# Moving the last query products ahead of the second probability turns, and masks and scores half by half, in a fused attention and mixture-of-experts kernel

## The chip, the cores and the metric

The kernel runs on one core of one Trainium2 chip. The metric is the device time of one execution in microseconds (us); lower is better. The profile is one execution of the same program, recorded by the hardware profiler.

## What is computed

`x` is 16 batches of 112 tokens of width 256. A cross-attention block against a context of 375 rows is added to `x` first. Then four layers follow. The part of a layer that matters here is causal self-attention with rotary positions, and after it a mixture of eight experts, of which each token uses two:

```python
for l in range(L):                       # L = 4, x is (16, 112, 256)
    h = rms(x) * ln1_w[l]
    q, k, v = h @ wq[l], h @ wk[l], h @ wv[l]     # 16 query heads, 4 key heads, head width 64
    q, k = rotate(q), rotate(k)                   # q * cos + rot_half(q) * sin
    a = softmax(q @ k.T / 8 + causal) @ v
    x = clip(x + a @ wo[l], -100, 100)
    h = rms(x) * ln2_w[l]
    comb = top_2(softmax(h @ wr[l]))              # 8 experts, 2 per token
    x = clip(x + sum_e comb[e] * ((silu(h @ wg[l][e]) * (h @ wu[l][e])) @ wd[l][e]), -100, 100)
```

## The kernel before, in words

Each engine has its own instruction list, written out by hand. Nothing is reordered; semaphores tie the lists together. Everything is float32, apart from the masks, which are bfloat16.

**A layer's attention** is a loop over the 16 batches on every engine (`iteration(b)` on TensorE and ScalarE, the loop `for b in range(B)` on VectorE, `attention(l)` on GpSimd). Projections are made for pairs of batches, `g = b // 2`. While pair `g` is attended, queries and keys of pair `g + 1` are projected: `heads_of(l, g + 1, m, bank)` (L819) makes key group `m = 0` and query groups 1 to 4. The even batch of a pair makes groups 0 and 1, the odd batch groups 2 (bank 0), 3 (bank 1) and 4 (bank 2). VectorE rotates each group (`rotate`: a shuffle L1628, two multiplications L1630 and L1632), and GpSimd adds the two halves of a query group (`add_rotated`, L594), which counts `g_rope`.

**One batch on TensorE**, in order: masks of heads 0 to 7 and of heads 8 to 15 (`causal`, L839, 4 matmuls each) and scores (`products`, L851, 16 matmuls each); the output projection of the batch before (`out_project`, L906, 16 matmuls); values (L827, even batches) or query group 2 (odd); the turns of probabilities 0 and 1 (`turn_probs`, L871, 4 transposes each, into banks 4 and 5); the turn of the residual rows (L891); the next projection; `turn_probs` 2 and 3, into banks 4 and 5 again; the router's logits (`route_logits`, L898); one more projection; in odd batches up to 11 the turn of the normalised input of pair `g + 2` (`norm_turn`, L810, into bank 4); and probabilities times values (`weigh`, L882).

`norm_turn` writes bank 4, so it waits until ScalarE has copied probability unit 2 out of that bank (`copy_probs`, L1300, which counts `a_pt`). `weigh` waits for the copies of all four units.

**One batch on VectorE**: the row maxima of each half of the scores (`maxima`, L1648), between them the sum of expert outputs for a later batch (`rows_in`, from the second layer on), the scaling of the first half of the probabilities (`scale_probs(b, 0)`, L1657 and L1658), the attention added to the residual (`add_attention`, L1663 and L1664), `scale_probs(b, 1)`, the rotations with the logits (`take_logits`, L1669) among them, and the two best experts (`top_two`). In batches 10 to 15 pieces of the routing come on top (`place_first`, `tiles_of_first` and others), which turn expert choices into row positions.

**One batch on ScalarE**: two output copies (L1304), 16 exponentials (L1291), the copies of turned probabilities (L1300), the copy of turned rows (L1317), in odd batches up to 11 the normalised input (`norm_in`, L1273), two more copies L1300, and a sum of squares (`square_out`, L1310).

**After the first nine batches** GpSimd scatters their rows to expert order in DRAM (L626, in batches 12, 13 and 14, between its additions L594). In batch 14 TensorE turns the first two expert tiles (`turn_tile`, L934), which SyncE loads once these scatters have landed.

## Time and profile before

| | |
|---|---|
| time before, median of 3 runs | 1882.78 us (1881.21 to 1884.82) |
| the profiled execution's own time | 1881.46 us |
| its span in the profile | 1879.6 us |
| TensorE (matmuls) busy | 1834.9 us, 98% of the span |
| VectorE busy | 1261.9 us, 67% |
| ScalarE busy | 950.8 us, 51% |
| GpSimd busy | 538.8 us, 29% |

A busy share says how much of the span the engine had an instruction in work. For TensorE, matmuls overlap and their ends are modelled, so the start of one group to the start of the next is the safer measure of what a group costs. The attention loops are at about 136 to 375 us, 570 to 806, 999 to 1235 and 1430 to 1666 us of the span; the expert tiles lie between them.

### The profile page before, as it was taken

To read this page: it belongs to the slowest core of one execution; us is meant where nothing else is said; L and a number is where in the kernel's file an instruction comes from. 1 tells how busy PE (TensorE), PEld (TensorE's weight loads), DVE (VectorE), ACT (ScalarE), POOL (GpSimd) and SP (SyncE) were. 2 spreads that over 40 slices of the span, in tenths; PEclk is the share of its full clock that TensorE was granted. 3 is DMA by queue.
4 is the path that set the end of the run, shared out by engine and by line. 5 is a ranking of instruction groups with operands and counts; after the bars stand their busy time and mean duration, and the time that the engine had idled before them with its cause. 6 is when DMAs were issued, how large, how long until landed. Compare 5 with 4: busy or idle time off the path is not lost.

```text
span 1879.6 us, 36506 instructions
## 1 busy us (share of the span) xinstructions
PE 1834.9 (98%) x10612; PEld 1360.0 (72%) x10613; DVE 1261.9 (67%) x3041; ACT 950.8 (51%) x3629; POOL 538.8 (29%) x721
## 2 busy tenths in 40 slices
PE   7999999999999999999999999999999999999995
PEld 5887888766668888766667888766667888865663
DVE  4676678754477878764566778764466778865456
ACT  4646777622226777732235777642224777752221
POOL 4652113440032332540032232531032332530024
PEclk9999999999999999999999999999999999999998
DMA  6423220256662330245562330235663431136566
GB/s 166 134 72 107 102 101 7 85 134 148 148 156 91 131 116 7 85 122 145 146 161 84 122 135 21 85 99 145 145 164 85 137 117 45 43 98 146 148 164 173
DMA packets 255292, 212.48 MB, mean 113 GB/s; under 512 B 145827, under 2 KB 226421, under 8 KB 255029
## 3 DMA queue, kind: packets, MB, share of 16 engines
q1 hardware_dynamic: 240808, 174.86, 33.8%
q0 software_dynamic: 13952, 35.33, 6.4%
q8 instruction: 82, 1.34, 0.3%
q14 instruction: 70, 0.57, 0.1%
q10 hardware_dynamic: 380, 0.38, 0.1%
HBM read 137.44 MB, written 73.05 MB: 112 GB/s over the span
## 4 chain that ended last, share of the span: by engine, by line
PE 87%; DVE 3%; DMA 3%; POOL 2%; ACT 2%; issue 2%; SPq 1%; POOLq 0%; DVEq 0%; ACTq 0%
PE ps L940 24%; PE ps L966 12%; PE ps L819 12%; PE ps L906 10%; PE ps L882 5%; PE ps L851 5%; PE ps L871 5%; PE ps L827 3%; PE ps L801 2%; ACT parena L1291 2%; PE ps L934 2%; PE ps L839 2%; PE ps L745 1%; PE ps L783 1%; PE ps L898 1%
## 5 line engine op out<-in xcount | busy, mean ns | idle before, releaser
L940 PE MATMUL ps<-arena,xeT 128*128 x1120 | 509.5, 593 | 0.0
L1291 ACT ACTIVATE parena<-ps,nmax 112x112 f32<-112x112 f32 x1024 | 345.5, 387 | 82.8 <-DVE nmax L1648 82.8
L940 PEld LDWEIGHTS ps<-arena,xeT 128*128 128x128 f32 x1120 | 210.2, 190 | 193.5 <-issue 187.3
L594 POOL TENSOR_TENSOR qk<-qk,rope 128x448 f32<-128x448 f32 x128 | 146.2, 1142 | 549.9 <-DVE rope L1632 549.8
L1345 ACT ACTIVATE parena<-ps,er 128x512 f32<-128x512 f32 x140 | 96.2, 687 | 375.6 <-PE ps L940 375.6
L819 PE MATMUL ps<-xnT,wqk_s 128*128 128x224 f32 x1280 | 273.5, 357 | 0.0
L573 POOL DMA_INDIRECT y_in<-sorted_y,pos x114 | 109.2, 958 | 499.6 <-DMA sorted_y<-tarena 397.4
L1291 ACT ACTIVATION_READ_ACCUMULATOR parena<-ps,nmax 112x1 f32 x1024 | 245.8, 240 | 0.0
L906 PE MATMUL ps<-wo_s,oT 128*112 128x256 f32 x1024 | 237.9, 385 | 1.3 <-issue 1.3
L819 PEld LDWEIGHTS ps<-xnT,wqk_s 128*128 128x128 f32 x1280 | 234.2, 191 | 2.4
L1932 DVE SCALAR_TENSOR_TENSOR parena<-parena,ps 128x512 f32<-128x512 f32 x140 | 96.1, 686 | 181.7 <-ACT parena L1345 181.6
L906 PEld LDWEIGHTS ps<-wo_s,oT 128*112 128x112 f32 x1024 | 175.7, 177 | 42.9 <-issue 2.0
L1648 DVE TENSOR_REDUCE nmax<-ps 112x8 f32<-112x896 f32 x128 | 136.8, 1086 | 58.7 <-PE ps L851 58.6
L626 POOL DMA_INDIRECT sorted_x<-x_sb,pos_x x128 | 124.2, 970 | 173.2 <-DVE pos_x L1855 139.5
L1335 ACT ACTIVATE xeT<-ps,ln2T 128x128 f32<-128x128 f32 x280 | 87.1, 364 | 170.5 <-PE ps L934 167.8
L966 PE MATMUL ps<-arena,tarena 128*128 x640 | 152.8, 382 | 2.3 <-issue 1.5
L1300 ACT ACTIVATE tarena<-ps 112x448 f32<-112x448 f32 x256 | 129.2, 574 | 37.4 <-PE ps L871 37.0
L1658 DVE TENSOR_TENSOR parena<-parena,rrec 112x896 f32<-112x896 f32 x128 | 139.8, 1092 | 4.4
L1934 DVE SCALAR_TENSOR_TENSOR parena<-parena,er,ps 128x512 f32<-128x512 f32 x140 | 104.7, 748 | 54.6 <-PE ps L940 54.0
L1304 ACT ACTIVATE oT<-ps 128x448 f32<-128x448 f32 x128 | 69.3, 545 | 120.7 <-PE ps L882 120.7
L966 PEld LDWEIGHTS ps<-arena,tarena 128*128 128x128 f32 x640 | 119.1, 195 | 14.8 <-issue 3.9
L851 PE MATMUL ps<-qk 64*112 64x112 f32 x2048 | 121.9, 262 | 0.0
(207 smaller groups left out, 2753.1 us busy)
## 6 DMA issues: line engine op xcount, KB each, us to landing
sorted_y<-tarena SPq DMA_DIRECT2D x140, 128.0 KB
xe<-sorted_x SPq DMA_DIRECT2D x132, 130.0 KB, 2.5
arena<-in_L_ffn_wg_dram SPq DMA_DIRECT2D x32, 512.0 KB, 3.7
arena<-in_L_ffn_wu_dram SPq DMA_DIRECT2D x32, 512.0 KB, 4.6
arena<-in_L_ffn_wd_dram SPq DMA_DIRECT2D x32, 512.0 KB, 5.6
hid_d<-tarena SPq DMA_DIRECT2D x240, 64.0 KB
tarena<-hid_d SPq DMA_DIRECT2D x60, 256.0 KB, 2.8
hid_d<-parena SPq DMA_DIRECT2D x240, 64.0 KB
```

The source lines that it names most:

```text
L573: pool.indirect_dma_start(out=y_in[:, b % 2, k, :], out_offset=None, in_=sorted_y[0:FIRST * SLOT, :] if b < PARTS[0][1] else sorted_y, in_ ...
L594: pool.tensor_tensor(q, q, rope[m % 2][:, :], ALU.add).then_inc(g_rope, 1)
L626: pool.indirect_dma_start(out=sorted_x if h == 0 else sorted_x[0:HROWS - WHOLE * SLOT, :], out_offset=bass.IndirectOffsetOnAxis(ap=pos_x[: ...
L819: last = pe.matmul(ps[:, bank, x * TN:x * TN + TN], wqk_s[:, k, n, :], xnT[:, g % 2, k, :], start=(k == 0), stop=(k == KD - 1))
L851: last = pe.matmul(score_out(b, p, j)[:, i, :], qT[g % 2][js, 4 * p + i, u * S:u * S + S], keys[g % 2][js, p, u * S:u * S + S], start=Fals ...
L906: last = pe.matmul(ps[0:S, 6, 0:D], oT[:, p, i * S:i * S + S], wo_s[:, 4 * p + i, :], start=(p == 0 and i == 0), stop=(p == 1 and i == 3))
L940: last = pe.matmul(ps[:, bank, :], xeT[u][:, k, :], w[:, bass.ds(e * 1024 + k * 512, 512)], start=(k == 0), stop=(k == KD - 1))
L966: last = pe.matmul(ps[:, 6, u * D:u * D + D], chunk, wd_s[:, bass.ds(e * 1024 + c * D, D)], start=(c == 0), stop=(c == 3))
L1291: last = act.activation(prob[:, n, :], ps[0:S, bank, h * S:h * S + S], ACT.Exp, bias=nmax[:, b % 2, n:n + 1], accum_out=rsum[:, b % 2, n:n ...
L1300: act.activation(probT[:, unit, :], ps[0:S, 4 + unit % 2, 0:GN], ACT.Copy).then_inc(a_pt, 1)
L1648: dve.tensor_reduce(nmax[:, b % 2, hs].rearrange("p (n h) -> p n h", n=2), heads(b, p), AX_X, ALU.max, negate=True).then_inc(d_max, 1)
L1658: dve.tensor_tensor(prob[:, hs, :], prob[:, hs, :], bc(rrec[:, hs], 2, [S, 8, S]), ALU.mult).then_inc(d_norm, 1)
```

## The change

In odd batches with a next pair, TensorE makes query group 4 and the logits before it turns probabilities 2 and 3. VectorE rotates group 2 before it scales the second half of the probabilities, then rotates group 3, takes the logits, and rotates group 4. ScalarE sums the squares before the second pair of copies. In all batches the masks and the scores go half by half; before, even batches up to 12 made both masks first and both halves of the scores after them. `place_first(1)`, in batch 11, comes after the second scaling instead of ahead of it.

```diff
@@ TensorE, iteration(b)
-                        together = not odd and b != B - 2
                         causal(b, 0)
-                        if not together:
-                            products(l, b, 0)
+                        products(l, b, 0)
...
                         causal(b, 1)
-                        if together:
-                            products(l, b, 0)
                         products(l, b, 1)
...
+                    if odd and more:
+                        pe.wait_ge(a_exp, l * 32 + 2 * b + 2)
+                        heads_of(l, g + 1, 4, 2)
+                        route_logits(b - 1)
                     turn_probs(b, 2)
                     turn_probs(b, 3)
-                    if b:
+                    if b and not (odd and more):
                         route_logits(b - 1)
-                    if more:
+                    if more and not odd:
                         pe.wait_ge(a_exp, l * 32 + 2 * b + 2)
                         if b:
-                            heads_of(l, g + 1, 4 if odd else 1, 2)
-                    else:
+                            heads_of(l, g + 1, 1, 2)
+                    elif not more:
@@ ScalarE, iteration(b)
+                    if odd and g + 1 < NP:
+                        square_out(b - 1)
                     copy_probs(b, 2)
                     copy_probs(b, 3)
...
-                    if b:
+                    if b and not (odd and g + 1 < NP):
                         square_out(b - 1)
@@ VectorE, the loop over b
+                    if odd and g + 1 < NP:
+                        rotate(step, l, g + 1, 2, 0)
+                    scale_probs(b, 1)
                     if b == RANK_STEP + 1:
                         place_first(1)
-                    scale_probs(b, 1)
...
                         if odd:
-                            rotate(step, l, g + 1, 2, 0)
+                            rotate(step, l, g + 1, 3, 1)
                         else:
                             rotate(step, l, g + 1, 0, 1 if b else 2, between=take_logits)
                     if b and (odd or g + 1 == NP):
                         take_logits(b - 1)
                     if g + 1 < NP:
                         if odd:
-                            rotate(step, l, g + 1, 3, 1)
+                            rotate(step, l, g + 1, 4, 2)
                         else:
                             rotate(step, l, g + 1, 1, 2 if b else 3)
-                    if odd and g + 1 < NP:
-                        rotate(step, l, g + 1, 4, 2)
```

## Rows read from the trace of the kernel before

**Rows 1.** The page's busy line: busy time, share of the span, instructions.

```profile
PE 1834.9 (98%) x10612; PEld 1360.0 (72%) x10613; DVE 1261.9 (67%) x3041; ACT 950.8 (51%) x3629; POOL 538.8 (29%) x721
```

**Rows 2.** Stretch view: batches 5, 6 and 12 (first layer), batch 12 (fourth).

```profile
core 0: us, PE busy (x) PEld busy (x) DVE busy (x) ACT busy (x) POOL busy (x), PEclk, DMA share, GB/s
214.62:229.22 14.60, 14.60 (x116) 12.50 (x114) 11.14 (x26) 10.50 (x46) 4.31 (x5) 1.00 0.32 109
229.22:243.69 14.47, 14.47 (x114) 11.86 (x112) 9.42 (x21) 10.87 (x47) 1.14 (x1) 1.00 0.31 110
317.45:332.24 14.79, 14.73 (x113) 11.77 (x112) 12.59 (x32) 10.47 (x45) 7.07 (x7) 1.00 0.14 41
1608.08:1623.10 15.02, 14.94 (x112) 11.74 (x110) 12.82 (x33) 10.48 (x45) 7.13 (x7) 1.00 0.13 40
```

**Rows 3.** Timeline of TensorE, batches 5 and 6: start, length, engine, line, count.

```profile
214.62 0.40 PE L839 MATMUL ps<-rows_b,causal_b 64*112 64x256 bf16 x4
...
216.74 3.71 PE L906 MATMUL ps<-wo_s,oT 128*112 128x256 f32 x16
220.28 1.68 PE L819 MATMUL ps<-xnT,wqk_s 128*128 128x224 f32 x8
...
222.80 1.69 PE L819 MATMUL ps<-xnT,wqk_s 128*128 128x224 f32 x8
224.33 0.93 PE L871 MATMUL ps<-cst,parena 112*112 112x112 f32 x8
225.10 0.47 PE L898 MATMUL ps<-wr_s,x2T 128*112 128x8 f32 x4
225.43 1.76 PE L819 MATMUL ps<-xnT,wqk_s 128*128 128x224 f32 x8
227.02 0.62 PE L810 MATMUL ps<-cst,xn 112*128 112x112 f32 x4
227.57 1.72 PE L882 MATMUL ps<-tarena,v_s 112*64 112x448 f32 x8
229.22 0.59 PE L839 MATMUL ps<-rows_b,causal_b 64*112 64x256 bf16 x8
229.65 1.85 PE L851 MATMUL ps<-qk 64*112 64x112 f32 x32
231.43 0.47 PE L906 MATMUL ps<-wo_s,oT 128*112 128x256 f32 x1
```

**Rows 4.** Timeline of GpSimd, end of batch 5: the addition of query group 4.

```profile
229.27 1.14 POOL L594 TENSOR_TENSOR qk<-qk,rope 128x448 f32<-128x448 f32 x1 [0.56 <-DVE rope L1632]
```

**Rows 5.** Timeline of ScalarE: copy of unit 2 alone, batch 5.

```profile
224.92 0.54 ACT L1300 ACTIVATE tarena<-ps 112x448 f32<-112x448 f32 x1 [0.21 <-PE ps L871]
```

**Rows 6.** Timelines, batch 0: ScalarE's copies and what they release on TensorE.

```profile
153.27 0.53 ACT L1300 ACTIVATE tarena<-ps 112x448 f32<-112x448 f32 x1
153.94 0.95 PE L871 MATMUL ps<-cst,parena 112*112 112x112 f32 x8 [1.26 <-ACT tarena L1300]
584.59 0.98 ACT L1300 ACTIVATE tarena<-ps 112x448 f32<-112x448 f32 x2 [1.32 <-PE ps L871]
585.62 0.20 PEld L882 LDWEIGHTS ps<-tarena,v_s 112*64 112x64 f32 x4 [0.56 <-ACT tarena L1300]
```

**Rows 7.** Timeline of VectorE, batch 5: second scaling and rotations 3 and 4.

```profile
222.83 1.09 DVE L1658 TENSOR_TENSOR parena<-parena,rrec 112x896 f32<-112x896 f32 x1
...
225.79 0.67 DVE L1628 STREAM_SHUFFLE rope<-ps 128x448 f32<-128x448 f32 x1
...
227.42 0.66 DVE L1628 STREAM_SHUFFLE rope<-ps 128x448 f32<-128x448 f32 x1
```

**Rows 8.** Timelines of VectorE and of TensorE's weight loads in batch 12.

```profile
319.47 1.09 DVE L1648 TENSOR_REDUCE nmax<-ps 112x8 f32<-112x896 f32 x1
323.44 0.70 PEld L827 LDWEIGHTS ps<-wv_s,xnT 128*112 128x112 f32 x4 [0.47 <-ACT parena L1291]
```

**Rows 9.** Timelines of GpSimd (batch 13) and TensorE (batch 14).

```profile
345.18 1.14 POOL L594 TENSOR_TENSOR qk<-qk,rope 128x448 f32<-128x448 f32 x1 [0.80 <-DVE rope L1632]
...
357.62 0.95 PE L934 MATMUL ps<-cst,xe 128*128 128x128 f32 x4 [0.32 <-DMA xe<-sorted_x]
358.51 0.97 PE L882 MATMUL ps<-tarena,v_s 112*64 112x448 f32 x4
```

## Prediction, made before the changed kernel ran

> **What bounds the kernel now.** The page's busy line comes first: TensorE has matmuls in work for 98% of the span, VectorE for 67% [rows 1]. That is a hint and no proof, so I read the stretches batch by batch, from the first mask of one batch to the first mask of the next. Batch 5 takes 14.60 us and batch 6 takes 14.47, and TensorE is busy for all of both, at granted clock 1.00 [rows 2]. The other engines rest for 3 us and more in each. So in a plain batch only two things move the time: what TensorE's own list costs from start to start, and a wait put into that list. VectorE, ScalarE and GpSimd matter only where they reach TensorE. Batch 12 shows the other kind: 14.79 us, 0.32 more than batch 6, and 15.02 in the fourth layer [rows 2]. All 64 batches follow these patterns; I count types and multiply.
>
> **Even batches, masks and scores half by half.** In batch 6 the 8 masks start at 229.22 and the output projection at 231.43: 2.21 us. In batch 5, which already goes half by half, the same 40 matmuls take 214.62 to 216.74: 2.12 us [rows 3]. No matmul is removed, so where are the 0.09? The second half of the scores needs GpSimd's addition of query group 4, which ends at 229.27 + 1.14 = 230.41 [rows 4]; the scores began at 229.65, and 16 of them at half of (231.43 - 229.65) would be through at 230.54. The first half at batch 5's pace would be through about 0.1 earlier. So the second half waits about 0.1 us for GpSimd. After the change the even batch does what batch 5 does, if group 4 is there in time: bounds 0 and 0.10 saved, I take 0.09 because the odd batch measures the same list. Six even batches a layer (2 to 12), four layers: 24 x 0.09 = 2.2 us saved. The wait on the first half is for groups 1 and 2, added long before. The maxima start earlier, but TensorE doesn't wait for them in plain batches: worth nothing.
>
> **Odd batches, order on VectorE.** Group 2's projection ends at 220.28 + 1.68 = 221.96 [rows 3], and a rotation occupies VectorE for 227.42 - 225.79 = 1.63 us [rows 7]. Ahead of the second scaling it runs from about 222.1 to 223.8; the scaling, which ended at 222.83 + 1.09 = 223.92 [rows 7], ends at about 225.1. The turn that waits for it used to start at 224.33; it now stands behind another projection of 1.53 (222.80 to 224.33) and the logits at 0.33 (225.10 to 225.43) [rows 3], so at 226.19. The scaling is ready 1.1 us before. Price if that cover were gone: up to 0.8 us a batch, the 225.1 against 224.33. Rotation 4 starts as soon as rotation 3 and the logits are taken, at about 226.8 instead of 227.42, so group 4 is added at about 229.7, while the next batch's second half of scores comes 1.2 us after a later batch start. No wait there.
>
> **Odd batches, order on TensorE.** Here I see a new wait. The turns of units 2 and 3 fill banks 4 and 5, and `norm_turn` fills bank 4 again. Before, logits and a projection (225.10 to 227.02, 1.92 us) lay between; after, nothing does. With S the start of the turns: ScalarE's copy of unit 2 started at 224.92, S + 0.59, and took 0.54 [rows 3, 5], so bank 4 is free at S + 1.13. TensorE would be through its eight turns at S + 0.77 (224.33 to 225.10) [rows 3]. The step from ScalarE's end to TensorE's start is bounded by batch 0: a copy from 153.27 of 0.53 ends at 153.80 and the turn starts at 153.94, 0.14 later; a pair that ends at 584.59 + 0.98 = 585.57 lets the weight load go at 585.62, 0.05 later [rows 6]. So `norm_turn` starts at S + 1.18 to S + 1.27.
>
> I cost the groups from the end of group 3's projection to `weigh` as a whole. Before, turns, logits, projection, `norm_turn`: 224.33 to 227.57, 3.24 us [rows 3]. After: projection 1.53, logits 0.33, then 1.18 to 1.27 to `norm_turn`, then its 0.55 (227.02 to 227.57) [rows 3]: 3.59 to 3.68. Logits followed by a turn instead of by a projection have no row; the projection behind the logits takes 1.59 (225.43 to 227.02) against 1.53, so up to 0.06 may hang on that junction. The difference is +0.35 to +0.50; I take +0.41, near the middle, as the longer step of 0.14 is that of the same pair of lines. Only odd batches 1 to 11 have a `norm_turn`: 6 x 4 x 0.41 = 9.8 us lost (8.4 to 12.0). Queued behind the wait are `weigh` and the next batch's masks and scores, so all of it is on the path. `weigh` itself isn't late: the second copy ends at about S + 1.6, and `weigh`'s units 2 and 3 start after S + 1.8. Batch 13 has no `norm_turn`: projection after projection saves the 0.06, 4 x 0.06 = 0.2 us.
>
> The Trainium skill, Perfetto Trace Analysis, section Matmuls, says that independent matmul groups should rotate through different PSUM banks, so that the copying out of one overlaps the matmuls of the next. It speaks against this edit, which lets two groups in bank 4 follow each other with one group between. Row and rule agree on the sign; the rule has no price, and without it the sum below is the same.
>
> ScalarE's sum of squares moves into time in which it waits for the turns: nothing.
>
> **Batch 12.** Its maxima start at 319.47, 2.02 us after the batch began at 317.45, while the first half of its scores would be done 1.2 us after that start at batch 5's pace. VectorE was behind with routing work, the exponentials followed late, and the values waited 0.47 us as a weight load [rows 8]. Since VectorE ends rotation 4 some 0.6 earlier against TensorE's list, and the batch starts 0.41 later, the delay goes, even with `place_first(1)` now uncovered (0.34): I expect 14.47 - 0.09. Beyond the 0.09 counted that is 0.32 in three layers (taking the first for them) and 0.55 in the fourth [rows 2]: 1.5 us saved (bounds 0 and 1.7).
>
> **Batch 14.** The expert tiles' turn starts at 357.62 after a wait for the load of `xe`, and ends only at 358.51: 0.89 for four transposes that cost about 0.55 as in `norm_turn`, with 0.32 or more of idle time ahead [rows 9]. The logits before them should take 0.33, and the whole is about 0.7 too long. The load waits for the last scatters, they for GpSimd, and GpSimd waited 0.80 us for VectorE's rotation 3 at 345.18 in batch 13 [rows 9]. That rotation comes about 0.77 earlier: it used to stand behind the scaling and rotation 2's own late start. So the scatters move 0.77 ahead and most of the wait goes: 4 x 0.68 = 2.7 us saved (bounds 0 and 3.0, as a transfer's time wanders).
>
> **Sum.** +9.8 - 2.2 - 0.2 - 1.5 - 2.7 = +3.2 us. The profiled execution took 1881.46 us for a span of 1879.6, so it would become 1884.7. It lies 1.3 below the median of the runs, 1882.78, against which the forecast is set: 1886.0 us. The expert part is untouched; its waits move with TensorE.
>
> **The rivals.** A difference of 0.2%, 3.8 us, is about what a measurement of this kernel can tell from no change.
> (a) The new wait, and nothing given back in batch 14: the tiles' load is bound by the DMAs and not by when the scatters were issued, and the junction costs its upper 0.06 too. For it: the load's time in the profile is that of two chained transfers. Against: GpSimd did wait on VectorE. 24 x 0.45 - 2.2 - 0.2 - 1.5 = +6.9: 1889.7 us. Chance 0.20.
> (b) The other side, faster: the wait at bank 4 isn't there, because ScalarE finds the copy ready sooner or TensorE's turns take longer behind the logits. Then the odd batch costs 0 and the savings stay: -6.6, 1876.2 us. It decides below 0.12 us of added time per odd batch, since 24 x 0.12 - 6.6 = -3.7. Against it stand the 0.59 and 0.54 of rows 3 and 5, which nothing in the change shortens. Chance 0.08.
> (c) A different wait: the scaling behind rotation 2 is late for the turns. It has 1.1 us of cover. If 0.2 of it showed in 28 odd batches, +5.6 on top: 1891.6. Chance 0.04.
> (d) Even batches keep their 2.21: +5.4, 1888.2. Chance 0.04.
> The forecast itself, within about 3 us of its time: 0.64.
>
> **How the numbers follow.** The forecast's own range, with the wait at its bounds (-1.4, +2.2) and the savings at theirs, is 1883 to 1889. To hold eight in ten it must reach (a) and most of (d) upward and allow the runs' spread downward: 1881.5 to 1891.0. Faster by over 0.2%: (b), 0.08. Slower: (a), (c) and (d), 0.28, and of the forecast the part above +3.8, which I put at 0.17 of its 0.64 although the centre is at +3.2, because a median of runs also moves by itself: 0.45 in all. Same: 0.47.
>
> **What the profile would show.** Right: in odd batches 1 to 11 a `norm_turn` (L810) with an idle bracket released by L1300, and 15.0 us for such a batch; even batches at 14.38; batch 12 without the weight load's wait; L934 in batch 14 with no or little wait for `xe`. Wrong: no bracket at L810, or one above 0.6 us; L871 waiting for L1658; the second half of an even batch's scores waiting for L594; batch 14 unchanged although L626 came earlier.

## The result, and the profile after

The changed kernel takes 1892.54 us (median of 9 runs, 1889.08 to 1897.17), the kernel before 1883.67 beside it (9 runs). The ratio is 1.0053, 95% interval 1.0041 to 1.0065. The forecast was 1886.0, with a range up to 1891.0: the sign was right, the size was not, and the time lies outside the range. The profiled execution took 1890.37 us for a span of 1888.5. It is 8.9 us longer than the span before, 1879.6.

The page's busy line of the changed kernel answers to [rows 1]:

```profile
PE 1838.0 (97%) x10612; PEld 1360.3 (72%) x10613; DVE 1276.7 (68%) x3041; ACT 950.8 (50%) x3629; POOL 542.8 (29%) x721
```

The instructions are the same in number, but VectorE is busy for 14.8 us more and GpSimd for 4.0 more. Nothing in the change gives them more work, so this line alone raises the question which of their instructions became longer.

The stretch view of the changed kernel shows batches 5, 6, 12 and 14 of the first layer, from first mask to first mask as in [rows 2]:

```profile
215.77:230.84 15.07, 14.82 (x116) 12.55 (x114) 11.97 (x27) 10.50 (x46) 4.57 (x6) 1.00 0.31 105
230.84:245.21 14.37, 14.37 (x114) 11.78 (x112) 9.27 (x19) 10.87 (x47) 0.89 (x1) 1.00 0.32 111
320.48:335.15 14.67, 14.62 (x114) 11.70 (x112) 12.52 (x31) 10.48 (x45) 7.03 (x7) 1.00 0.14 41
349.24:363.03 13.79, 13.10 (x109) 10.06 (x107) 7.36 (x21) 10.51 (x47) 7.62 (x8) 1.00 0.27 82
```

The granted clock (the share of full speed at which TensorE was allowed to run, the number before the DMA share) is 1.00 in all four, as before. I took the same difference for all 64 batches, after less before:

| batches (times four layers) | forecast, each | measured, each |
|---|---|---|
| 1, 3, 5, 7, 9 | +0.41 | +0.47 |
| 11 | +0.41 | +0.77 |
| 2 to 10, even | -0.09 | -0.10 |
| 12 | -0.41, in layer 4 -0.64 | -0.11, in layer 4 -0.36 |
| 13 | -0.06 | -0.05 |
| 14 | -0.68 | -0.06 in the mean (+0.02, -0.43, +0.11, +0.06) |
| sum of all 64 | +3.2 | +9.45 |

The rest of the 8.9 is scatter in the start and the expert parts. The plain batches came out nearly as forecast. Batches 11, 12 and 14 didn't: the first cost more than it should, and the other two gave almost nothing back.

TensorE's timeline in batch 5 of the changed kernel:

```profile
223.96 3.21 PE L819 MATMUL ps<-xnT,wqk_s 128*128 128x224 f32 x16
227.00 0.47 PE L898 MATMUL ps<-wr_s,x2T 128*112 128x8 f32 x4
227.32 0.95 PE L871 MATMUL ps<-cst,parena 112*112 112x112 f32 x8
228.53 0.73 PE L810 MATMUL ps<-cst,xn 112*128 112x112 f32 x4 [0.25 <-ACT tarena L1300]
229.19 1.72 PE L882 MATMUL ps<-tarena,v_s 112*64 112x448 f32 x8
```

This is the wait that was forecast, with the releaser that was forecast. From the start of the turns to `norm_turn` it takes 228.53 - 227.32 = 1.21 us (forecast 1.18 to 1.27). But from there to `weigh` it takes 0.66, where [rows 3] has 0.55. The list of waits (us in total, times, longest) has it in all 24 odd batches up to 11:

```profile
PE ps L810 <- ACT tarena L1300: 6.0, 24, 0.3
```

VectorE and GpSimd in the same batch show what was not forecast (the scaling is L1660 now):

```profile
225.18 2.02 DVE L1660 TENSOR_TENSOR parena<-parena,rrec 112x896 f32<-112x896 f32 x1
...
228.74 0.15 DVE L1671 COPY lg<-ps 112x8 f32<-112x8 f32 x1
```

```profile
225.11 1.13 POOL L594 TENSOR_TENSOR qk<-qk,rope 128x448 f32<-128x448 f32 x1 [6.84 <-DVE rope L1634]
```

The second scaling took 1.09 in [rows 7] and takes 2.02 here, in each odd batch up to 11. GpSimd's addition of group 2 starts 0.07 before it and ends at 226.24. The scaling ends at 227.20, 0.96 after that. It looks as if it did nearly nothing while the addition ran. The change itself brought them together: the rotation now ends right before the scaling, and the end of the rotation is what releases the addition.

In batch 14 the same instruction meets another one. GpSimd's and VectorE's timelines, and the chain that released the expert tile's turn:

```profile
353.58 0.94 POOL L626 DMA_INDIRECT sorted_x<-x_sb,pos_x  x1 [0.30 <-issue]
354.82 1.84 POOL L626 DMA_INDIRECT sorted_x<-x_sb,pos_x  x1 [0.30 <-issue]
```

```profile
354.77 1.09 DVE L1660 TENSOR_TENSOR parena<-parena,rrec 112x896 f32<-112x896 f32 x1
```

```profile
354.82 3.46 DMA sorted_x<-x_sb,pos_x
358.28 0.02 issue
358.30 2.11 DMA xe<-sorted_x
360.41 0.14 issue
360.54 0.91 PE ps L934 x4
```

The last scatter takes 1.84 us where the one ahead of it takes 0.94. It lands 3.46 after it was issued. Before, that was 2.78, with the scatter itself at 1.15. Here the scaling came first, and it looks as if the scatter had to stand behind it.

The Trainium skill, page "SBUF — State Buffer", section "Who interferes with whom", says that a VectorE `tensor_tensor` with both inputs in SBUF and a GpSimd instruction that reads SBUF want the same port pair, that whoever starts first has it for the whole instruction, and that the other does nothing meanwhile. The rows above have that form: 2.02 is 1.06 beside the addition and 0.96 after it. The rows show the times; that the operands are the reason had to be tested.

### The profile page after: what moved, and what is told of

It is laid out like the page before. It is cut to its first block, busy times and chain, and to the rows that moved or that the text cites. A ratio compares the mean times of both kernels' runs of the same rounds, so it can differ in the third digit from the quotient of the medians.

```text
span 1888.5 us, 36506 instructions
## 1 busy us (share of the span) xinstructions
PE 1838.0 (97%) x10612; PEld 1360.3 (72%) x10613; DVE 1276.7 (68%) x3041; ACT 950.8 (50%) x3629; POOL 542.8 (29%) x721
## 4 chain that ended last, share of the span: by engine, by line
PE 87%; DVE 4%; DMA 2%; issue 2%; POOL 2%; ACT 1%; SPq 1%; POOLq 0%; DVEq 0%; ACTq 0%
PE ps L940 25%; PE ps L966 13%; PE ps L819 11%; PE ps L906 11%; PE ps L882 5%; PE ps L851 5%; PE ps L871 4%; PE ps L827 3%; PE ps L801 2%; PE ps L934 2%; PE ps L839 2%; PE ps L745 1%; PE ps L783 1%; PE ps L810 1%; PE ps L898 1%
## 5 line engine op out<-in xcount | busy, mean ns | idle before, releaser
L819 PE MATMUL ps<-xnT,wqk_s 128*128 128x224 f32 x1280 | 266.6, 355 | 0.0
L1660 DVE TENSOR_TENSOR parena<-parena,rrec 112x896 f32<-112x896 f32 x128 | 162.0, 1266 | 4.4
L871 PE MATMUL ps<-cst,parena 112*112 112x112 f32 x1024 | 120.2, 260 | 2.5 <-ACT tarena L1300 1.3
```

What stands on the lines that cost most here:

```text
L819: last = pe.matmul(ps[:, bank, x * TN:x * TN + TN], wqk_s[:, k, n, :], xnT[:, g % 2, k, :], start=(k == 0), stop=(k == KD - 1))
L871: last = pe.transpose(ps[0:S, 4 + j, i * S:i * S + S], prob[:, p * 8 + j * 4 + i, :], ident[0:S, 0:S])
L1660: dve.tensor_tensor(prob[:, hs, :], prob[:, hs, :], bc(rrec[:, hs], 2, [S, 8, S]), ALU.mult).then_inc(d_norm, 1)
```

## The experiments

Sixteen runs were made, of fifteen kernels. In each, "before" is the kernel before on the same chip. Theory A is the wait for bank 4. The others are named as they came up; the letter G stands for one thing in experiment 2 and for another in experiments 10 and 11. Where batches are compared, all four layers are meant unless one is named.

**1. The halves alone.** The kernel before with the masks and scores of even batches half by half:

```diff
-                        together = not odd and b != B - 2
                         causal(b, 0)
-                        if not together:
-                            products(l, b, 0)
+                        products(l, b, 0)
...
-                        if together:
-                            products(l, b, 0)
```

> The kernel before with only the even batches' masks and scores half by half. Theory A (the loss is the new wait at bank 4, halves are a small gain): 24 even batches shorter by about 0.10 us, the batch stretch 14.36 or 14.37 instead of 14.47, odd batches unchanged at 14.60; in all 2.4 us less than before, a ratio of 0.9987, which the timing may just not resolve. Theory B (going half by half costs, for instance because the first half is now closer to its producers): even batches 14.47 or more, time not below before.

Measured: 1881.93 against 1882.87, ratio 0.9996 (0.9987 to 1.0005). The even batches 2 to 8 stay at 14.45 to 14.48, so the expected 14.37 didn't come. TensorE's timeline of batch 6 in this run:

```profile
230.43 0.36 PE L839 MATMUL ps<-rows_b,causal_b 64*112 64x256 bf16 x4
230.64 1.04 PE L851 MATMUL ps<-qk 64*112 64x112 f32 x16
231.61 2.63 PE L906 MATMUL ps<-wo_s,oT 128*112 128x256 f32 x11
```

The second half of the scores takes 0.97 to the output projection where batch 5 of the kernel before takes 0.90 (215.84 to 216.74). The output projection still starts 2.21 after the batch, as before, and GpSimd's addition of group 4 still starts 0.05 after it and ends at 1.18. The halves cost nothing and give nothing.

**2. The moves alone.** The changed kernel with the even batches' masks and scores in their old order (the diff above, reversed).

> The changed kernel with the even batches' masks and scores as they were before (both masks first). The run with halves alone moved nothing, so theory F (the 0.10 us that even batches gained comes from query group 4 being added sooner, which the moved rotations bring, and not from the halves) expects 14.37 in even batches here too, odd batches at 15.07, and the time of the changed kernel. Theory G (it takes both edits together) expects even batches at 14.47 and 2.4 us more than the changed kernel.

Measured: 1892.94 against 1884.47, ratio 1.0047 (1.0033 to 1.0061). The even batches are 0.11 shorter here too, with the old order; the odd ones are at +0.47 and +0.77. GpSimd's addition of group 4 starts 0.25 ahead of batch 6 instead of 0.05 after it. So the 0.10 of the even batches is real and comes from the rotations that end sooner, not from the halves. The halves are worth nothing in either kernel. One layer differs: in the first, batch 14 is at -0.71. There the last scatter started 0.04 after the scaling instead of 0.06 to 0.10, and it took 0.93 and the scaling 1.16. Whether batch 14 gives its 0.7 back hangs on some hundredths here.

**3. GpSimd's addition after the scaling.** The changed kernel, in odd batches:

```diff
                             if odd and m == 2:
+                                pool.wait_ge(d_norm, l * 32 + 2 * b + 2)
                             add_rotated(l, g + 1, m)
```

> The changed kernel, but GpSimd's addition of query group 2 waits until VectorE's second scaling of that odd batch is done. Theory C (the 2.02 us of that scaling, 1.09 before, come from GpSimd's addition running beside it): the scaling falls back to 1.09 in all odd batches, VectorE is 0.9 us earlier behind it, batch 11 loses its extra 0.30 us (15.38 to 15.08), batch 12 loses its wait of about 0.30 (14.67 to 14.37), plain odd batches stay at 15.07. Sum 4 x 0.6 = 2.4 us less than the changed kernel. Theory D (the scaling is slow for another reason, such as the rotation just ahead of it): it stays at about 2.0 us and nothing moves.

Measured: 1892.19 against 1882.87, ratio 1.0042 (1.0028 to 1.0055). VectorE and GpSimd in batch 5 of this run:

```profile
227.57 1.09 DVE L1662 TENSOR_TENSOR parena<-parena,rrec 112x896 f32<-112x896 f32 x1
```

```profile
228.74 1.14 POOL L594 TENSOR_TENSOR qk<-qk,rope 128x448 f32<-128x448 f32 x1 [8.10 <-DVE parena L1662]
```

The scaling is back at 1.09. In all four layers batch 11 falls from +0.77 to +0.47, and batch 12 from -0.11 to -0.41 (in the fourth from -0.35 to -0.65). Together that is the 2.4 us that theory C expected. The plain odd batches stay at 15.07 and batch 14 stays as it was. So the long scaling accounts for batches 11 and 12, and it does nothing in the plain odd ones while the wait for bank 4 stands there.

**4. The turned rows in bank 3.** The changed kernel with the wait for bank 4 taken away: `norm_turn` writes bank 3, whose scores have been read by then, ScalarE copies it at the end of the odd batch, and the next batch's second masks wait for that copy.

```diff
-                        pe.wait_ge(a_pt, l * 64 + b * 4 + 3)
+                        pe.wait_ge(a_exp, l * 32 + 2 * b + 2)
                         for k in range(KD):
-                            norm_turn(l, g + 2, k, 4, k * TN)
+                            norm_turn(l, g + 2, k, 3, k * TN)
...
```

> The changed kernel, but the turn of the normalised input goes to bank 3, whose scores are used up, and ScalarE copies it out at the end of the odd batch instead of in the next one. Theory A (the loss is the wait for bank 4): the wait at L810 is gone, odd batches 1 to 9 fall from 15.07 to about 14.55, 24 x 0.5 = 12 us less than the changed kernel, so 2 to 4 us below the kernel before. Theory E (the loss is the moved projection or the new neighbours on TensorE, not the bank): odd batches stay near 15 us. If the copy out of bank 3 is late for the next batch's masks, even batches show a wait of a few tenths at L839.

Measured: 1892.07 against 1882.87, ratio 1.0047 (1.0034 to 1.0061). TensorE in batch 5 of this run:

```profile
227.66 0.96 PE L871 MATMUL ps<-cst,parena 112*112 112x112 f32 x8
228.46 0.64 PE L810 MATMUL ps<-cst,xn 112*128 112x112 f32 x4
229.33 1.72 PE L882 MATMUL ps<-tarena,v_s 112*64 112x448 f32 x8 [0.24 <-issue]
```

`norm_turn` follows the turns after 0.80 and waits for nothing. But `weigh` now waits: it overwrites the bank of the logits, and VectorE, held up by its long scaling, takes them only at 229.08 to 229.23. The plain odd batches cost +0.27 instead of +0.47. A second wait stood 0.2 us behind the first. The 12 us that theory A expected became 4.0 by these batches, and the time shows even less; in the profiled execution batch 14 of the fourth layer is 2.9 us longer than before (see what stays open).

**5. Both.** Experiments 3 and 4 in one kernel.

> Both of the last two edits. Theories A and C together: odd batches about 14.55 with batch 11 like the others, even batches 14.37 with batch 12 like the others; about 14 us below the changed kernel and 4 to 6 us below the kernel before, ratio to before about 0.997. If the two costs are not separate (the freed time is lost to the same wait), it is no faster than the one with bank 3 alone.

Measured: 1881.36 against 1882.87, ratio 0.9993 (0.9984 to 1.0002). The odd batches are at 14.57, 0.03 below the kernel before, the even ones 0.10 below, batch 12 0.24. The 64 batches sum to -1.9 where the changed kernel had +9.45. In batches 1 to 13, which the fourth layer's batch 14 doesn't blur, it is -4.3 against +9.6: 13.8 us less. There the two edits alone gave 2.4 (experiment 3: 0.6 per layer in batches 11 and 12) and 4.0 (experiment 4: 0.20 in each of 20 plain odd batches). So the whole loss is gone with the two together, and more than half of it goes only so. The expected ratio of 0.997 was missed for two reasons. Batch 12 gets 0.24 and not the 0.41 of experiment 3: batch 11 is 0.50 shorter, so VectorE is nearer to being late, its maxima start 1.78 after the batch (1.32 in experiment 3), and the values wait 0.34. And batch 14 gives nothing back and is 2.65 longer in the fourth layer. The same kernel ran again beside experiment 9:

> The same kernel as bank3_pool, beside late_scaling_14 on one chip, so that the two are compared directly. By the earlier run: ratio to before 0.9993, all odd batches at 14.57, batch 14 as before.

Measured: 1881.17 against 1882.77, ratio 0.9991 (0.9982 to 0.9999). The batches repeat, apart from batch 14: +1.50, +1.08, +0.01 and +1.05.

**6. Logits between the turns and `norm_turn`.** The changed kernel with `route_logits` behind `turn_probs(b, 3)` in all batches.

> The changed kernel, but the router's logits come back between the last two turns and the turn into bank 4 (odd batches). Theory A (the wait is for the copy of unit 2 out of bank 4): the 0.33 us of the logits fill most of it, the idle time at L810 falls from 0.25 to about 0 and plain odd batches from 15.07 to 14.75 or a little above, since the logits are then taken later by VectorE; 24 x 0.3 = 7 us less than the changed kernel at most. If the next wait behind it (the probabilities times values waiting for the logits to be taken) takes over, odd batches stay within 0.15 of 15.07. Theory E (no wait, only dearer neighbours): no change.

Measured: 1889.86 against 1884.47, ratio 1.0031 (1.0021 to 1.0040). The plain odd batches stay at +0.42. TensorE and VectorE in batch 5 of this run:

```profile
225.81 3.21 PE L819 MATMUL ps<-xnT,wqk_s 128*128 128x224 f32 x16
229.10 0.98 PE L871 MATMUL ps<-cst,parena 112*112 112x112 f32 x8
229.92 0.47 PE L898 MATMUL ps<-wr_s,x2T 128*112 128x8 f32 x4
230.33 0.73 PE L810 MATMUL ps<-cst,xn 112*128 112x112 f32 x4
```

```profile
227.03 2.02 DVE L1659 TENSOR_TENSOR parena<-parena,rrec 112x896 f32<-112x896 f32 x1
```

The logits fill 0.33 of the time in which bank 4 is awaited: from the turns to `norm_turn` it is still 1.23. But the turns start 3.29 after the projections instead of 3.04, since the scaling ends at 229.05 and they come 0.33 sooner than in the changed kernel. With the scaling at 1.09 they would have gone 0.25 earlier. In batch 13, with no `norm_turn` to fill, `weigh` now waits 0.30 for the logits (+0.28).

What the plain odd batches gain over the changed kernel (0.05 each), batch 13 loses again. This kernel's ratio is 1.0031 where the changed one had 1.0053, and that is batch 14: it is at -0.71, -1.14, -0.69 and -0.71. GpSimd and VectorE in the first layer's:

```profile
356.33 0.93 POOL L626 DMA_INDIRECT sorted_x<-x_sb,pos_x  x1 [0.30 <-issue]
```

```profile
356.81 1.09 DVE L1659 TENSOR_TENSOR parena<-parena,rrec 112x896 f32<-112x896 f32 x1
```

The last scatter starts 5.04 after the first mask of batch 14, where the changed kernel has 5.58, and so 0.48 ahead of the scaling (0.34 in the fourth layer). It keeps its 0.93, and the expert tile's turn waits for nothing. Nothing is left out of this kernel and the operands are the same: only the order in which the two instructions start has changed.

**7. The cover taken away.** TensorE has the order of the kernel before, VectorE and ScalarE that of the changed one, so that the scaling stands behind rotation 2 and no projection 4 covers it.

> TensorE's odd batches in the order of before (turns, logits, projection of group 4, turn into bank 4), halves in all batches, VectorE and ScalarE in the order of the changed kernel. Rival (c) of the prediction: the rotation ahead of the second scaling makes the turns of units 2 and 3 wait, because nothing covers it. With the scaling at 2.02 us, ended at 12.6 us less its start (about 11.4 us after the batch began) against turns at 9.7, the wait is 1.5 to 1.7 us in each of 28 odd batches, about 40 us over the kernel before; with a scaling of 1.09 it would be 0.8 and 22 us.

Measured: 1926.63 us in a single run, span 1924.8. TensorE in batch 5:

```profile
228.96 1.69 PE L819 MATMUL ps<-xnT,wqk_s 128*128 128x224 f32 x8
232.24 0.98 PE L871 MATMUL ps<-cst,parena 112*112 112x112 f32 x8 [1.59 <-DVE parena L1656]
```

The turns start 3.28 after the projection instead of 1.53: 1.75 late, and the whole is 42 us over the kernel before, where about 40 was expected. In batch 13, where the scaling takes 1.09, they are 0.83 late. That is the "0.8" that the prediction gave as the price of the lost cover. It is right where the two engines don't meet and less than half where they do.

**8. The scaling of batch 14 left out.** The changed kernel in which the first half of batch 14's probabilities is not multiplied by its reciprocals (that part of the computation is left out).

> The changed kernel without the multiplication that scales the first half of the probabilities in batch 14 (that half stays unscaled, so the output is not the reference's). Theory H (the last scatter before the expert tiles takes 1.84 us instead of 1.15 because VectorE's scaling, which reads two SBUF operands, runs beside GpSimd writing its descriptors): the last L626 of the first nine batches falls to about 0.95, its data land about 0.9 us sooner, TensorE's wait at L934 goes and batch 14 is about 0.7 shorter (13.8 to 13.1). Rival (the scatter is long for its DMA or its rows): it stays at 1.8.

Measured: 1887.98 us in a single run, span 1886.1. GpSimd and TensorE in batch 14:

```profile
354.76 0.93 POOL L626 DMA_INDIRECT sorted_x<-x_sb,pos_x  x1 [0.30 <-issue]
```

```profile
359.62 0.47 PE L898 MATMUL ps<-wr_s,x2T 128*112 128x8 f32 x4
359.95 0.70 PE L934 MATMUL ps<-cst,xe 128*128 128x128 f32 x4
```

The scatter takes 0.93, the tile's turn waits for nothing, and batch 14 is 0.72, 1.03, 0.69 and 0.71 shorter than before. That is the 0.68 that the forecast had counted on, and the same as in experiment 6.

**9. The scaling of batch 14 behind the last scatter.** Experiment 5, with a semaphore that GpSimd raises after the last scatter and for which VectorE waits ahead of that scaling.

> The kernel of bank3_pool, and in batch 14 the scaling of the first half of the probabilities waits until GpSimd has issued the last scatter of expert rows. Theory H (the last scatter is slow because the scaling, which reads two operands in SBUF, runs beside it): the last scatter falls from 1.75 to about 0.95 us, the rows land 0.8 us earlier, the first expert tiles' turn has no wait left, batch 14 loses 0.6 to 0.7 us in each of the four layers, as it did when the scaling was left out, and the whole is 2.5 us below bank3_pool (which stood at 1881.4 beside a before of 1882.9), so about 1879 us, ratio to before 0.998. Rival J (the wait is handed on: the scaling ends up to 1 us later, and the turns of the first half of the probabilities or the attention added to the residual come late): batch 14 shows a wait in front of L873 or of the output projection of batch 14 or 15 instead, and the sum stays within 0.5 us of bank3_pool. Which of the two is read from batches 14 and 15 together.

Measured: 1881.56 against 1882.77, ratio 0.9996 (0.9985 to 1.0007), and batch 14 at -0.04, -0.41, +0.14 and +3.28, much as in experiment 5. VectorE and GpSimd in this run:

```profile
351.03 1.09 DVE L1668 TENSOR_TENSOR parena<-parena,rrec 112x896 f32<-112x896 f32 x1
```

```profile
351.18 1.75 POOL L629 DMA_INDIRECT sorted_x<-x_sb,pos_x  x1 [0.31 <-issue]
```

The scaling ran just ahead of the scatter all the same. The reciprocal that stands behind the same wait ran at 350.80, 0.38 before the scatter: the semaphore had risen by then. So this run tells nothing about either theory.

**10. The reciprocals in PSUM.** All of these moved or left out work. The next three change where one operand lies, and add the waits that this needs: the reciprocals go to 16 spare columns of PSUM bank 4, so that the scaling reads one operand in SBUF and one in PSUM. One kernel is the changed one, one is experiment 4, one is the kernel before.

```diff
+        rrec_p = ps[0:S, 4, 448:448 + NH]
...
+                    if b:
+                        r = rrec_p
+                        dve.wait_ge(a_pt, l * 64 + b * 4 + (1 if p else -1))
...
-                    step(dve.reciprocal(rrec[:, hs], rsum[:, b % 2, hs]))
-                    dve.tensor_tensor(prob[:, hs, :], prob[:, hs, :], bc(rrec[:, hs], 2, [S, 8, S]),
+                    step(dve.reciprocal(r[:, hs], rsum[:, b % 2, hs]))
+                    dve.tensor_tensor(prob[:, hs, :], prob[:, hs, :], bc(r[:, hs], 2, [S, 8, S]),
```

> The changed kernel with one thing different: the reciprocals by which the probabilities are scaled lie in 16 spare columns of PSUM bank 4 instead of in SBUF (from batch 1 on), so that the scaling reads one operand in SBUF and one in PSUM. No order on any engine is changed. Theory G (a VectorE instruction with two operands in SBUF and a GpSimd instruction hold each other up): the second scaling of odd batches goes back from 2.02 to about 1.09 us although GpSimd's addition of group 2 still starts just before it, batch 11 loses its extra 0.30, batch 12 its wait, and the last scatter in batch 14 lasts about 0.95 us with its 0.7 us per layer regained: 0.3 + 0.3 + 0.7 for four layers is 5 us, so a ratio of about 1.003 (1888 us). The plain odd batches stay at 15.07, as in pool_after_scale, since the wait of L810 for bank 4 stays. Rival K (the scaling is slow because it runs behind the rotation on VectorE, or because memory in SBUF is shared with the DMAs): it stays at 2.02 and nothing else moves. Rival M (an operand in PSUM is slow to read): 1.09 becomes more everywhere, and the batches get longer.

> The same on top of bank3 (the turn of the normalised rows in bank 3). By theory G this has all that bank3_pool regained, and batch 14 besides: odd batches at 14.57, even ones at 14.37, batch 12 as 6, batch 14 shorter than before by 0.7 us: -2.4 - 1.0 - 0.7 - 2.8 is -7 against the kernel before, so about 1876 us, ratio 0.996. If GpSimd's addition itself is slower or comes later in another place, or if batch 14's load does not follow the scatter, the ratio is 0.999, as with bank3_pool.

> The kernel before with the reciprocals in PSUM alone. There the scaling runs beside GpSimd only in batches 13 and 14: the last scatter took 1.10 to 1.15 us and would take 0.95, batch 14 loses at most 0.2 us per layer, the rest stays: ratio 1.000 to 0.9995. If it gains as much as bank3_recip_psum, the gain of that kernel is not the change's but the operand's.

Measured: 1959.19, 1947.80 and 1971.05 us against 1931.14, ratios 1.0144, 1.0089 and 1.0209. All three are much slower. VectorE and GpSimd in batch 5 of the first, and VectorE in its batch 6:

```profile
226.94 1.09 DVE L1667 TENSOR_TENSOR parena<-parena,ps 112x896 f32<-112x896 f32 x1
...
241.55 0.21 DVE L1666 RECIPROCAL ps<-rsum 112x8 f32<-112x8 f32 x1 [1.68 <-ACT tarena L1301]
```

```profile
226.86 1.16 POOL L595 TENSOR_TENSOR qk<-qk,rope 128x448 f32<-128x448 f32 x1 [6.84 <-DVE rope L1635]
```

The two instructions run side by side at full speed, which is what the theory says. But the edit carried a wait of its own. In an even batch the second reciprocal stands behind ScalarE's copy out of bank 4, 1.68 us, and the turns behind it: +0.35 and more per even batch. Batches 13 and 14 are 3 to 6 us longer, and there more is at work than that wait. The stretch view of batch 13 and ScalarE's timeline in it:

```profile
339.08:358.87 19.79, 16.67 (x113) 12.51 (x112) 12.76 (x34) 9.51 (x42) 11.96 (x12) 0.89 0.35 113
```

```profile
351.91 0.98 ACT L1301 ACTIVATE tarena<-ps 112x448 f32<-112x448 f32 x2 [4.50 <-remote]
```

The profile names no engine of this core as the releaser of that copy ("remote"), and the granted clock falls to 0.5 (1.2 GHz) for 6.8 us from 354.4. TensorE had waited 2.62 just before. Both stand in batch 13 of every layer of all three kernels, and in none of experiment 11. The kernel before took 1931 us beside them, 48 more than beside any other experiment, with a mean granted clock of 0.984 to 0.988 in its nine runs where it otherwise had 0.992 or more. There is no trace of it from there. So what slowed all four is open, the edit's own part in batches 13 and 14 isn't known, and the sizes tell nothing about the theory.

**11. The reciprocals in two banks.** The same, with those of the second half in bank 3, whose scores have been read when they are written (in batches 0, 10 and 14 they stay in SBUF). The added waits are for copies made long before. The diff is against experiment 10 in its first lines.

```diff
-        rrec_p = ps[0:S, 4, 448:448 + NH]
+        rrec_p = [ps[0:S, bank, 448:448 + NH] for bank in (4, 3)]
...
+                    if p == 0 and b:
+                        r = rrec_p[0]
...
+                    elif p and b not in (0, RANK_STEP, MID_STEP, B - 2):
+                        r = rrec_p[1]
```

> recip_in_psum without the wait that it had put in: in even batches its second reciprocal stood behind ScalarE's copy out of bank 4 (1.7 us), and TensorE's turns 0.25 behind that. Here the reciprocals of the first half lie in bank 4, which has long been copied then, and those of the second half in bank 3, whose scores have been read. Theory G: the second scaling of odd batches takes 1.09 us although the addition of group 2 starts just before it (recip_in_psum showed 1.09 beside an addition of 1.16 us), batch 11 is back at 15.07, batch 12 at 14.37, the last scatter at about 0.95 and batch 14 shorter than before by 0.7: ratio about 1.003. Rival N: what the scaling gains, the addition or the scatter loses, or another wait of VectorE stands in the same place: ratio as the changed kernel's, 1.005.

> The same on top of bank3. Theory G: odd batches 14.57, even ones 14.37, batch 12 as 6, batch 14 shorter by 0.7: -2.4 - 1.0 - 0.7 - 2.8 is -7 us against the kernel before, ratio 0.996. Rival N: 0.999 or more.

> The kernel before with the reciprocals in the same two places. The last scatter goes from 1.10 to 1.15 to 0.95 and batch 14 loses up to 0.2 us per layer, all else stays: ratio 0.9995 to 1.000. If it gains as much as bank3_psum_two, that kernel's gain is the operand's and not the change's.

Measured, against 1882.51: 1886.73, ratio 1.0023 (1.0014 to 1.0032); 1876.21, ratio 0.9965 (0.9951 to 0.9978); 1881.75, ratio 0.9994 (0.9985 to 1.0003). The expected ratios were 1.003, 0.996 and 0.9995 to 1.000. VectorE, GpSimd and TensorE of the first of them, batch 5, and GpSimd's last scatter and TensorE in batch 14:

```profile
226.45 1.09 DVE L1669 TENSOR_TENSOR parena<-parena,ps 112x896 f32<-112x896 f32 x1
```

```profile
226.37 1.15 POOL L595 TENSOR_TENSOR qk<-qk,rope 128x448 f32<-128x448 f32 x1 [6.84 <-DVE rope L1635]
...
355.50 0.93 POOL L627 DMA_INDIRECT sorted_x<-x_sb,pos_x  x1 [0.30 <-issue]
```

```profile
228.59 0.95 PE L872 MATMUL ps<-cst,parena 112*112 112x112 f32 x8
229.79 0.73 PE L811 MATMUL ps<-cst,xn 112*128 112x112 f32 x4 [0.25 <-ACT tarena L1301]
230.46 0.97 PE L883 MATMUL ps<-tarena,v_s 112*64 112x448 f32 x4
...
360.68 0.70 PE L935 MATMUL ps<-cst,xe 128*128 128x128 f32 x4
```

The addition still starts 0.08 before the scaling, and both are at their full speed, with the rotation just ahead as before: that speaks against rivals K and M, and the ratio against N. With nothing else changed, batch 11 is at +0.47 and batch 12 at -0.41, -0.41, -0.42 and -0.65. Batch 14 is at -0.71, -1.14, -0.48 and -0.63. The 64 batches sum to +4.25, where the changed kernel had +9.45.

The stretch view of the second, with `norm_turn` in bank 3 as well, batches 5, 6, 12 and 14:

```profile
217.02:231.59 14.57, 14.57 (x117) 12.51 (x115) 11.20 (x28) 11.17 (x48) 5.00 (x6) 1.00 0.32 110
231.59:245.95 14.36, 14.36 (x112) 11.78 (x110) 9.10 (x18) 10.19 (x45) 0.48 (x1) 1.00 0.34 111
319.42:333.96 14.54, 14.54 (x112) 11.69 (x110) 12.70 (x31) 9.80 (x43) 6.76 (x7) 1.00 0.14 42
348.06:361.12 13.06, 12.76 (x109) 9.90 (x107) 7.38 (x21) 10.51 (x47) 6.73 (x8) 1.00 0.30 86
```

Its 64 batches sum to -7.3 us against the kernel before. It is the one version that is clearly faster than the kernel before. Batch 12 is at -0.24 here too, not as batch 6. The operand alone gives the kernel before 1.4 us by its batches (batch 14: -0.15 to -0.58), which the times can't tell from nothing, so most of the 7 belongs to the change, once both of its waits are gone.

## Why the prediction failed, point by point

**The wait at bank 4: right, mis-sized by 0.06.** The step was "3.59 to 3.68", taken as +0.41 per odd batch. Measured: projection 1.52, logits 0.32, 1.21 to `norm_turn`, 0.66: 3.71, so +0.47. Its first term held (1.21 in 1.18 to 1.27): the copy starts at S + 0.61, takes 0.54, and `norm_turn` follows 0.06 after it. The last, "then its 0.55", did not: four transposes that start after a wait take 0.66 to the next group's start, here and in experiment 11, where the logits had long been taken, and 0.57 to 0.58 in the kernels with bank 3 where `weigh` doesn't wait. That is 24 x 0.06 = 1.4 us. That the wait sets these batches is shown by experiments 3 and 5, and again by the two kernels of experiment 11: without the long scaling they are at 15.07 with the wait and 14.57 without it.

**The failed step: "a rotation occupies VectorE for 1.63 us ... the scaling ... ends at about 225.1".** The scaling was priced at the 1.09 of [rows 7], where GpSimd was idle. In the new order it runs beside GpSimd's addition of group 2, which the rotation ahead of it releases, and takes 2.02. The prediction looked at what each engine does and who waits for whom. It didn't ask what the neighbour engine would be doing in the place to which an instruction moves. Everything that came out wrong by more than 0.06 follows from it:

- Batch 11: +0.30 on top, 4 x 0.30 = 1.2 us. `weigh` waits for logits that VectorE, late by 0.93 and with `place_first(1)` to do, takes late. (From that instruction's start to the next it is 0.48, where the prediction had 0.34.) Experiments 3 and 11 take the 0.30 away in all four layers.
- Batch 12: "the delay goes" is wrong for the changed kernel. The maxima still start 1.90 us after the batch (322.38 - 320.48), and the values wait 0.46 as a weight load, as in [rows 8]. 1.2 us of saving is missing. With the scaling at 1.09 the delay goes as forecast: -0.41 and -0.65 (experiments 3 and 11).
- Batch 14: "the scatters move 0.77 ahead and most of the wait goes". They did move ahead, by 0.74 against batch 13's start. But that put the last scatter under the scaling (354.82 against 354.77), it took 1.84 instead of 1.15, and the rows landed at the same time as before: 23.13 us after that start instead of 23.19. 2.5 us of saving is missing. Experiments 6, 8 and 11 give it back, in three ways: another order of the two, no scaling, another operand.

1.4 + 1.2 + 1.2 + 2.5 is 6.3, which is the difference between +3.2 and +9.45. With the collision taken out (experiment 11) the sum is +4.25; the forecast's +3.2 and the mis-sized wait make 4.6.

**Even batches: right in size and in mechanism, credited to the wrong part.** The prediction said that the second half waits for GpSimd's group 4, and made the halves the cure, "if group 4 is there in time". Experiments 1 and 2 show that being there in time is all of it.

**The cover of the rotation: the price "0.8" holds only without the collision.** It is 0.83 in batch 13 and 1.75 in the others (experiment 7). The cover sufficed, though barely: the scaling ended at 227.20, 0.12 before the turns started at 227.32, where 1.1 us had been forecast.

**The range: narrower than its own bounds.** The prediction gives 1883 to 1889 "with the wait at its bounds and the savings at theirs". Its bounds add up to more: +12.0 with all of the savings but batch 13's at nothing is +11.8, so 1894.6, and the low end is 1883.9. The measured 1892.54 lies within that. The range that was set, up to 1891.0, left no room for two savings to fail together, which they did, for one reason.

**The rivals.** (a) gave 1889.7 for "nothing given back in batch 14". That happened, but for another reason: the load is not bound by the DMAs, it followed as soon as the scatter was quick. (b) is excluded by the bracket at L810 in all 24 odd batches up to 11. (c) was worth asking for, but in the changed kernel no turn waited; it became true in experiment 6. (d) is excluded by 14.37.

**What stays open.** In the fourth layer the load of `xe` took 3.27 to 3.65 us instead of about 2.1 in all four runs that had `norm_turn` in bank 3 and the last scatter under the scaling (experiments 4, 5, its repeat, and 9). The tile's turn then waited 1.58 to 1.95; in no other run of the document did it wait more than 0.44. Where the granted clock then fell to 0.5 as well (experiments 4, 5 and 9), batch 14 was 2.65 to 3.28 longer; the repeat lost 1.50 and 1.08 in its first two layers to the clock alone. Why the load was slow isn't known. Nor is what slowed the kernel before to 1931 us beside experiment 10.

## What to carry to other kernels

When an instruction is moved, look at what the other engines will be doing at its new time, not only at who waits for it. Here a VectorE instruction with two operands in SBUF was placed right behind the one that releases a GpSimd instruction, and met it in every odd batch up to 11. Operands can be moved instead of work: 16 columns of PSUM took the collision away, and the scaling was no slower for it (but the columns must be free by then, as experiment 10 shows). And waits that stand 0.2 us apart hide each other, so undo them one by one and then together: here the two edits gave 2.4 and 4.0 us alone and 13.8 together.

## What the runs showed of the hardware

A 112x896 multiplication of two SBUF operands on VectorE takes 1.09 us alone and 2.02 when a 1.13 us addition on GpSimd starts 0.07 before it. If VectorE starts first, GpSimd pays: its addition takes 1.42 in batch 13, where it starts 0.41 before the scaling's end, and an indirect scatter 1.84 instead of 0.94. With one of the operands in PSUM all three keep their times (experiment 11): 1.09 for the multiplication, 1.15 for the addition and 0.93 for the scatter. And a semaphore that GpSimd raised behind an indirect scatter in its list had let VectorE go at 350.80, before the scatter began at 351.18. In that form it doesn't put work after a scatter.

The Trainium skill, page "SBUF — State Buffer", section "Who interferes with whom", has the rule for the multiplication and the addition, and the traces agree in kind: the loser's extra time is 0.93 for 1.06 of overlap. The start was 0.41 before the end in batch 13, and the extra time there was 0.28. The scatter, when it starts second, shows the same: 0.90 for 1.04, and 0.21 for 0.35 in the kernel before. So in each case the loser pays 0.13 to 0.14 less than the overlap.

One thing doesn't fit that section's rule, that the first has the ports for its whole instruction. When the scatter starts 0.08 to 0.48 ahead of the scaling (experiments 6 and 7), the scaling still takes 1.09, or 1.14 in one case. An addition that starts 0.07 ahead costs it 0.93. When the scatter starts 0.04 after the scaling, they take 0.93 and 1.16 (experiment 2, once); from 0.05 after on the scatter pays in full. So a scatter that comes first costs this multiplication next to nothing.
